# Stage two of a mixture-of-experts kernel: the late slots' expert numbers are loaded inside the products of slots 5 to 9, with no range check

## The reference

```python
# stage one: 4 experts, chosen by the token number
x = x + where(expert_ids == e, (silu(h @ C[e].T) * (h @ C[e].T)) @ C[e], ...)    # h = layernorm(x)
# stage two: 8 experts, chosen by a router; weights ternary, activations in 8 bits
idx = argmax(layernorm(x) @ router_w.T)
y = bitlinear(square(relu(bitlinear(h, wg[e]))) * bitlinear(h, wu[e]), wd[e])     # for rows with idx == e
x = x + y
```

## Time and profile before

| | |
|---|---|
| median of 3 runs | 247.66 us (247.25 to 249.02) |
| the profiled execution | 248.08 us |
| its span | 246.3 us |
| mean granted TensorE clock | 0.996 |
| TensorE matmuls busy | 217.4 us (88%) |
| VectorE, ScalarE busy | 208.3 us (85%), 198.1 us (80%) |
| stage two | from about 168 us to the end |

### The profile page before, as it was taken

The page is one execution under the profiler, slowest core; times in us unless marked ns, Lnnn a source line. Parts: engine busy times, 40 slices in busy tenths (PEclk is TensorE's granted clock), DMA queues, the critical chain, the costliest instruction groups (busy, mean ns, idle before and its releaser), DMA issues.

```text
span 246.3 us, 6303 instructions
## 1 busy us (share of the span) xinstructions
PE 217.4 (88%) x1622; PEld 169.4 (69%) x1629; DVE 208.3 (85%) x696; ACT 198.1 (80%) x297; POOL 162.6 (66%) x324
## 2 busy tenths in 40 slices
PE   2398989999999999999999999987669998899970
PEld 2245778889899999999999998975324444344430
DVE  5979989958969899899998999979799997788771
ACT  2777899868768899999999988996687988778860
POOL 5263567748737598888897887554735878566762
PEclk9999999999999999999999999999999999999998
DMA  5999999995975375788666676425238899992120
GB/s 192 428 313 391 421 424 382 404 366 204 396 271 174 110 249 200 259 314 301 207 202 211 232 247 221 174 85 176 55 92 258 256 314 383 395 376 110 63 109 13
DMA packets 14273, 61.44 MB, mean 249 GB/s; under 512 B 2654, under 2 KB 2654, under 8 KB 9632
## 3 DMA queue, kind: packets, MB, share of 16 engines
q1 hardware_dynamic: 9600, 47.60, 53.3%
q0 software_dynamic: 4640, 13.44, 15.6%
HBM read 43.88 MB, written 12.70 MB: 230 GB/s over the span
## 4 chain that ended last, share of the span: by engine, by line
PE 65%; DVE 17%; DMA 7%; issue 7%; ACT 1%; POOL 0%; DVEq 0%; ACTq 0%
PE banks L1834 31%; PE banks L2014 15%; PE banks L1817 6%; DMA staged<-weight_chunks 5%; PE banks L2016 5%; PE banks L2003 3%; DMA x<-x_rows,gather 2%; PE banks L1979 2%; DVE stats L1249 2%; PE banks L1859 2%; DVE row L1305 2%; DVE hT_lo L1278 1%; DVE h L1271 1%; DVE p L1285 1%; PE banks L1887 1%
## 5 line engine op out<-in xcount | busy, mean ns | idle before, releaser
L833 ACT ACTIVATE ternary<-staged 128x2048 bf16<-128x2048 f32 x20 | 38.1, 1906 | 2.6 <-DMA staged<-weight_chunks 2.6
L839 ACT ACTIVATE ternary<-staged,w_scale 128x1536 int16<-128x1536 f32 (+1 forms) x20 | 34.4, 1726 | 2.9 <-DVE w_scale L1202 2.9
L2014 PE MATMUL banks<-ternary,qT 128*128 x126 | 31.7, 379 | 1.8 <-ACT qT L922 1.6
L692 POOL DMA_INDIRECT x_rows<-row,store_at x19 | 22.6, 1188 | 9.0 <-POOL store_at L684 6.8
L594 POOL DMA_INDIRECT x<-x_rows,gather x16 | 18.4, 1148 | 9.1 <-DVE gather L1120 6.3
L1834 PE MATMUL banks<-ctx_hi,pT_hi 128*128 x132 | 22.9, 313 | 1.6 <-DVE row L1305 1.1
L647 POOL TENSOR_TENSOR row<-ln,half_powers 128x2 f32<-128x2 f32 x19 | 14.4, 759 | 13.0 <-DVE squares L1320 13.0
L1834 PE MATMUL banks<-ctx_hi,hT_hi 128*128 x132 | 22.8, 311 | 0.0
L1834 PE MATMUL banks<-ctx_lo,hT_hi 128*128 x132 | 21.2, 300 | 0.2 <-DVE ctx_lo L1149 0.2
L1834 PE MATMUL banks<-ctx_hi,pT_lo 128*128 x132 | 21.4, 301 | 0.0
L1834 PE MATMUL banks<-ctx_lo,pT_hi 128*128 x132 | 21.3, 300 | 0.0
(11 more groups left out here) (284 smaller groups left out, 640.0 us busy)
## 6 DMA issues: line engine op xcount, KB each, us to landing
staged<-weight_chunks SPq DMA_DIRECT2D x20, 1024.0 KB, 6.6
twin<-ternary SPq DMA_DIRECT2D x4, 1536.0 KB, 10.1
ternary<-ctx_chunks SPq DMA_DIRECT2D x4, 1024.0 KB, 8.3
ternary<-weight_chunks SPq DMA_DIRECT2D x4, 1024.0 KB, 9.6
ternary<-ctx_rows SPq DMA_DIRECT2D x4, 1024.0 KB, 14.5
late_rows<-x_rows SPq DMA_DIRECT2D x11, 260.0 KB, 3.1
x_rows<-filler SPq DMA_DIRECT2D x1, 2080.0 KB, 12.8
staged<-x_rows SPq DMA_DIRECT2D x5, 260.0 KB, 3.5
```

The costliest lines, as they stand in the source:

```text
L692: pool.indirect_dma_start(x1_rows, bass.IndirectOffsetOnAxis(ap=store_at[b % ROWS][:, :], axis=0), row[b % ROWS][:, :], None, bounds_check ...
L833: nc.scalar.activation(ternary[:, m * K * D:(m + 1) * K * D], staged_of(i), ACT.Abs, accum_out=abs_sum[:, 2 * i:2 * i + 1]).then_inc(abs_r ...
L839: nc.scalar.activation(ternary[:, m * K * D + first:(m + 1) * K * D].bitcast(I16), staged_of(i)[:, first:], ACT.Copy, scale=w_scale[:, m:m ...
L2014: last = pe.matmul(ps[:, :], rows, ternary[:, columns], start=(k == 0), stop=(k == K - 1))
```

## The change

Three things. First, all twenty loads of an expert number in stage two are made without the check of the range. Second, the loads for slots 6 to 19 leave their place behind the up product. Third, they are made in turns 5 to 9, one in the middle (between k = 1 and k = 2) of each product: in turn u, `gate_product(u)` loads the number of slot 6 + 3(u - 5), `up_product(u)` the next, `down_product(u - 3)` the one after. That is three loads in each of turns 5 to 8 and two in turn 9 (18 and 19). Turns 10 to 19 hold none. Slots 0 to 5 are loaded where they were.

```diff
                 place = b if b < EARLY else b - EARLY
-                ffn_expert[b] = pe.value_load(expert2[b >= EARLY][place:place + 1, 0:1], min_val=0, max_val=E2 - 1)
+                ffn_expert[b] = nc.values_load(expert2[b >= EARLY][place:place + 1, 0:1],
+                                               engines=(mybir.EngineType.PE,), min_val=0, max_val=E2 - 1,
+                                               skip_runtime_bounds_check_because="the tables hold experts alone")
...
+            def next_experts(b, kind):
+                after = EARLY + 1 + 3 * (b - EARLY) + kind
+                if b < EARLY or after >= B2:
+                    return None
+                return lambda: load_ffn_expert(after)
...
-                product2(g_ps[b % 2], qT[b % 2], b, 0).then_inc(g_ready, 1)
+                product2(g_ps[b % 2], qT[b % 2], b, 0, ahead=next_experts(b, 0)).then_inc(g_ready, 1)
...
-                product2(u_ps[b % 2], qT[b % 2], b, 1).then_inc(u_ready, 1)
+                product2(u_ps[b % 2], qT[b % 2], b, 1, ahead=next_experts(b, 1)).then_inc(u_ready, 1)
...
-                ahead = None
+                ahead = next_experts(b + 3, 2)
                 if b == B2 - 1:
...
                 up_product(u)
-                load_ffn_expert(u + 1)
+                if u < EARLY:
+                    load_ffn_expert(u + 1)
...
             up_product(B2 - 2)
-            load_ffn_expert(B2 - 1)
             transpose_r(B2 - 4)
```

## The result

The changed kernel took 250.89 us (median of nine runs, 249.28 to 252.63) against 248.01 us (nine runs, 247.16 to 249.02): ratio 1.0107, 95% interval 1.0077 to 1.0136. It is slower by 1%, 2.9 us. I had forecast +0.3 us and a range up to 250.3 us. A second measurement on another occasion gave 1.0062 (1.0026 to 1.0098), +1.9 us by the medians; the two intervals meet, and the loss lies between some 2 and 3 us. The profiled execution is the fastest of the nine, 249.28 us, 1.2 us above the profiled one of before.

What follows compares the result with a forecast made beforehand. TensorE's sequencer was taken as the bound. A loss of 4.1 us in turns 5 to 9, plus 0.1 for a restart, less 3.89 gained in turns 10 to 15, gave +0.3 us: 248.0 us, range 246.3 to 250.3 (8 in 10).

Steps and rivals of the forecast that it cites:

- its sum: TensorE's sequencer time from gate 5's first address instruction to up 9's last: 9.36 + 5.04 + 3.1 = 17.5 us.
- the 2.03 us of a turn: Time TensorE's sequencer needs for one turn without any load, against 2.81 us for the array.
- the 0.36 of a load: Sequencer time for one register load without check in turns 5 to 9: 0.30 us plus one step between instructions.
- The check: Removing it with loads in their old places: 0.27 us at slot 4 plus 1.7 us in turns 10 to 15, 2.0 us.
- The check at slot 4: At slot 4's load the check is on the path; without it, turn 4 and what hangs on it come 0.27 us earlier.
- L: Length of one register load on TensorE's sequencer: 0.30 us normally, longer in the slow stretch, 3.1 us extra over loads 14 to 19.
- the stretch of the twins: Time of four 1536 KB twin transfers, issued from 196.30 us on, when register loads take about 1 us.
- The gain: Turns 10 to 15 lose their loads and go at 2.81 us each: 3.89 us, less 0.1 for one restart.
- the ends of L: Loads 16 to 19: 0.7 us less or 1.4 us more in all; loads 12 to 15: 0.7 us more.
- A: Rival: no gaps in turns 5 to 7 although the loads are there; faster by over 1%; chance 0.10.
- B: Rival: loads packed into products cost about 0.60 us even before the slow stretch, adding 2.7 us: 250.7 us; chance 0.05.
- C: Rival: the 151 ns instruction belongs to the read and stays; every load costs 0.21 us more: 251.1 us; chance 0.06.

## Why the prediction was wrong

**The mechanism was right.** The bound is TensorE's sequencer. With the loads at 0.30 us its sum came out (14.4 us for 14.5), which confirms the 2.03 us of a turn and the 0.36 of a load together. The check came out at 2.1 us for 2.0. The array's floor is 2.81 and turns 10 to 15 reach it (16.9 us for 16.9 from up 9's last matmul to up 15's). The check at slot 4 gave 0.3 us for 0.27: from up 4 to gate 5 it took 5.4 us in both traces of before and 5.1 in both of the changed kernel.

**The step that failed is the size of L**, "I take 0.1 and 0.15 us over 0.30 for 14 and 15, 0.5 for 16, and 0.75, 0.8, 0.8 for 17 to 19: 3.1 us". Measured over fourteen times 0.30 us: 4.0 and 5.4 us in the two traces. Turns 5 to 9 took 18.2 and 19.6 us for 17.6 (the 17.5 of the sum, and 0.1 from the last address instruction to its weight load), and the surplus of 0.6 and 2.0 us is within 0.4 of that of the loads. Two things were missing. I priced the stretch of the twins only. In the first trace its price was right: loads 14 to 19 are 3.1 us over, as summed, though in other shares (16 took 1.1 us and not 0.8, 14 and 15 nothing extra). The 0.9 us beyond it are the loads of slots 8 and 13 alone, at 189.8 and 195.4. A load some 2 us behind the start of a scatter is dear too, and the earlier trace rows had one at 195.3, which I used only as a bound on loads 12 to 15. TensorE's own loads ahead of 196 us had missed that moment: those at 188.7 and 194.1 started 1.0 and 1.2 us behind a scatter's start and took 0.30. And the edge of the slow stretch moves: in the second trace SP issued the first twin at 195.78, in the first at 197.69, and six loads were dear at the end, not four.

**The gain was read from one trace.** 3.89 us is right for it. In the second trace of before, two of the six loads were short and the loss there only 2.6 us. With 2.6 to 3.9 us of gain, 0.3 for the check at slot 4 and 5.3 to 6.7 us of loss, the net is between 1 and 4 us; the two measurements say 2.9 and 1.9. The range ended at 250.3, 0.6 us short: I had worked out the ends of L for each load, but as though all else stayed in its place, and let the largest term of the gain stand without a range. One of these ends was also added up wrong: 0.60 us for loads 12 to 15 is 0.95 us more than the sum had for them, not 0.7.

**What stays open.** The lengths of the loads, in both kernels, account to within 1 us for the two traced executions (1.2 and 2.9 us over the traced ones of before), both at a granted clock of 0.993 or more. Fourteen of the changed kernel's 21 runs had a lower clock and a median 2.2 us longer, and none of them was traced. The forecast had no term for this. The seven runs at the high clock, median 249.3 us, lie inside the range.

**The rivals.** A is out: the gaps inside the products are there, 3.4 us of them, and the sequencer stops for a read whose value is not wanted for a turn. C is out: the 151 ns instruction was the check's. B is out as put (the median of the loads ahead of 196 us is 0.30), though it named the place where part of the loss was. By the Trainium skill, page "DMA: Bandwidth & Descriptors", section "Latency and other measured facts", a tensor_load takes at least about 600 ns; the fourteen loads of 298 to 308 ns disagree with it as a floor.

## What to carry to other kernels

When an engine's queue runs ahead of it, cost the queue's processor as an engine of its own: sum its instructions per turn, and place register loads where the sum stays under the engine's turn (here two a turn, not three). A register load's price depends on what the DMA engines do at that moment, so moving loads out of one traffic pattern needs a look at the traffic where they go. Where a forecast is the difference of two large terms, each term needs its own range, from more than one trace if there are some.

## What the runs showed of the hardware

A load of one number from SBUF into a register of TensorE's or SP's sequencer took 0.27 to 0.31 us when no transfer out of SBUF was under way, mostly 0.8 to 1.5 us beside SBUF-to-SBUF copies of 1536 KB, and up to 1.0 us some 2 us behind the start of a scatter of 128 rows to HBM. Not every load there was dear (334 ns at 206.9 beside the twins, 309 ns at 196.8 behind a scatter). Transfers from HBM into SBUF at the same time did not slow it (fourteen loads of 298 to 308 ns with the half transfers under way). That the common path is a read port of SBUF was not tested. In the trace of the moved loads with their check the granted clock was at half, 1.2 GHz, in three stretches: within 183 to 187, and twice more behind the 16 us in which the array had long gaps and was busy for 11.6:

```profile
183.00:187.00 4.00, 3.67 (x11) 1.50 (x12) 3.79 (x15) 1.80 (x5) 0.89 (x2) 0.57 0.84 223
187.00:203.00 16.00, 11.60 (x61) 5.05 (x60) 9.66 (x22) 10.89 (x21) 8.15 (x15) 1.00 0.92 277
203.80:207.20 3.40, 3.22 (x10) 1.04 (x9) 1.01 (x4) 0.60 (x2) 1.82 (x4) 0.50 1.04 403
214.00:217.40 3.40, 3.18 (x10) 1.48 (x11) 2.67 (x6) 1.21 (x2) 0.52 (x1) 0.51 1.06 344
```

The first of these has a price that the traces show. It lies where PE is busy, and from up 2 to gate 5 it took 15.5 us. The trace with the rows held back has a low stretch there too (183.6 to 187.0) and took 15.6 us. The other twelve took 13.9 to 14.1 us, eight of them with a low stretch between 176 and 182. For the two later stretches no run tells the clock's share from that of the loads, and why the stretch falls early or late was not tested.
